# Segment attention of a two-layer kernel: a round's projection and the MLP of the round before it are issued between other work

## The reference

```python
xn = rms_norm(x, attn_norm_w)
q, k, v = split(xn @ to_qkv_w)
q, k = rope(q), rope(k)                      # t * cos + rh * sin, rh: neighbours swapped
kf, vf = [k_extra, pm, k], [v_extra, pm, v]  # prefix: memory and persistent tokens
probs = softmax(where(mask, q @ kf.T * DH**-0.5, -1e30))
x = x + (probs @ vf).merge_heads() @ to_out_w
a, g = split(rms_norm(x, ff_norm_w) @ ff_w1 + ff_b1)
x = x + silu(g) * a @ ff_w2 + ff_b2
```

## Time and profile before

| | us |
|---|---|
| median of 3 runs | 1343.94 |
| lowest and highest | 1338.87, 1344.26 |
| profiled execution: time, span | 1345.08, 1343.3 |
| segment stage's rounds in it | 997.1 to 1305.96 |
| last MLP | 1305.96 to 1343.3 |

### The profile page before, as it was taken

One profiled execution on the slowest core, in us unless ns is written; L12 is line 12 of the kernel. 1 busy time (PEld: TensorE's weight loads), 2 busy tenths in 40 slices (PEclk: granted clock), 3 DMA queues, 4 the chain that ended last, 5 costly groups with the idle time before them and its releaser, 6 DMA issues. The chain is left out here.

```text
span 1343.3 us, 38339 instructions
## 1 busy us (share of the span) xinstructions
PE 1169.8 (87%) x15980; PEld 795.3 (59%) x15980; DVE 928.7 (69%) x1742; ACT 747.0 (56%) x1029; POOL 847.5 (63%) x1227
## 2 busy tenths in 40 slices
PE   3888855899999999999999999998766887879775
PEld 2555544566666666666666666665443746456472
DVE  6778764777777777778787878777266375674632
ACT  2333333477777777777777777776512435344251
POOL 2455538878787878787888888851028294572830
PEclk9999866899999999999999999999877888989885
DMA  6200003323232323232223232211000000000000
GB/s 170 70 0 0 0 0 108 119 69 107 83 107 69 119 72 114 77 102 89 100 77 112 79 104 86 71 60 37 4 14 1 1 1 10 0 8 2 8 2 7
DMA packets 70398, 75.88 MB, mean 56 GB/s; under 512 B 21308, under 2 KB 64956, under 8 KB 70108
## 3 DMA queue, kind: packets, MB, share of 16 engines
q1 hardware_dynamic: 70236, 73.57, 17.3%
HBM read 32.90 MB, written 0.92 MB: 25 GB/s over the span
## 5 line engine op out<-in xcount | busy, mean ns | idle before, releaser
L928 DVE TENSOR_REDUCE tops_sb<-ps_b 112x2 f32<-112x1000 f32 x384 | 460.4, 1199 | 158.4 <-PE ps_b L778 155.7
L874 ACT ACTIVATE probs_sb<-ps_a 128x896 f32<-128x896 f32 x352 | 322.7, 917 | 118.5 <-PE ps_a L759 118.5
L750 PE MATMUL ps_d<-probs_sb,values_sb 128*32 128x112 f32 x6144 | 229.1, 267 | 0.6 <-ACT probs_sb L874 0.5
L778 PE MATMUL ps_b<-keys_sb,queries_sb 64*112 64x500 f16 x768 | 164.8, 420 | 16.6 <-DVE tops_sb L928 9.8
L217 POOL TENSOR_SCALAR context_sb<-context_sb,ln_sb 125x128 f32<-125x128 f32 x384 | 166.2, 449 | 7.6 <-POOL ln_sb L235 7.5
L750 PEld LDWEIGHTS ps_d<-probs_sb,values_sb 128*32 128x32 f32 x6144 | 135.5, 110 | 40.3 <-issue 7.5
L759 PEld LDWEIGHTS ps_a<-queries_sb,keys_sb 64*128 64x128 f16 x3072 | 125.2, 102 | 48.8 <-ACT probs_sb L874 8.1
L759 PE MATMUL ps_a<-queries_sb,keys_sb 64*128 64x112 f16 x3072 | 141.2, 210 | 4.7 <-ACT probs_sb L874 4.1
L806 PE MATMUL ps_c<-xs_t_sb,w_kv_sb 128*128 128x200 f32 (+1 forms) x384 | 127.4, 430 | 0.0
L815 PE MATMUL ps_c<-w_kv_sb,xs_t_sb 128*128 128x128 f32 x768 | 122.0, 297 | 5.1 <-ACT k_rows_sb L891 5.1
L815 PEld LDWEIGHTS ps_c<-w_kv_sb,xs_t_sb 128*128 128x128 f32 x768 | 97.9, 195 | 27.5 <-issue 21.9
(11 more groups left out here) (258 smaller groups left out, 1949.9 us busy)
## 6 DMA issues: line engine op xcount, KB each, us to landing
keys_sb<-k_split_sb SPq DMA_DIRECT2D x288, 125.0 KB, 2.5
context_sb<-in_ctx SPq DMA_DIRECT2D x32, 750.0 KB
queries_sb<-q_split_sb SPq DMA_DIRECT2D x24, 112.0 KB, 5.6
keys_sb<-in_ones SPq DMA_DIRECT2D x3, 375.0 KB, 4.5
w_qk_sb<-in_w_qkv SPq DMA_DIRECT2D x1, 1024.0 KB, 12.3
queries_sb<-shift_sb SPq DMA_DIRECT2D x64, 1.8 KB
x_all_sb<-in_x SPq DMA_DIRECT2D x2, 448.0 KB
queries_sb<-in_zeros SPq DMA_DIRECT2D x8, 112.0 KB, 5.5
```

The source lines that it names most:

```text
L750: last = nc.tensor.matmul(o_bank[32 * (g % 4):32 * (g % 4) + 32, 112 * (g // 4):112 * (g // 4) + 112], values[r][:, k, g, :], probs[k % 2] ...
L778: last = nc.tensor.matmul(ps_b[0:2 * T, 512 * e:512 * e + 500], queries_of(b + d, e, g), keys[(r + d) % 3][64 * e:64 * e + 64, g, 500 * u: ...
L874: nc.scalar.activation(probs[s % 2][:].rearrange("p (e n) -> p e n", e=2), halves(ps_a[:, :]), ACT.Exp).then_inc(Q["probs_ready"], 1)
L928: nc.vector.tensor_reduce(tops[(b + d) % 2][:, :, n // 3, n % 3], ps_b[0:2 * T, :].rearrange("p (e n) -> p e n", e=2)[:, :, 0:500], axis=A ...
```

## The change

Each engine's `emit` is taken apart into functions that are called in another order. A round is now scores and softmax first; then 16 steps n, in which stand slice n of the projection of round i + 1, the turned and weighted probabilities and the output of round i by the tables below, and the MLP of round i - 1. The value products of a round stand between its scores. Ahead of the loop stand the projection, turn and values of round 0, behind it the MLP of the last round. In the blocks below the removed lines are left out; they stand in the kernel above.

```diff
-UP_AT, HT_AT, DOWN_AT = (4, 8, 12), 3, 15
+TURNED = {0: ((0, 0), (0, 1)), 1: ((0, 2), (0, 3)), 2: ((1, 0), (1, 1)), 3: ((1, 2), (1, 3)), 5: ((2, 0), (2, 1)),
+          6: ((2, 2), (2, 3)), 8: ((3, 0), (3, 1)), 9: ((3, 2), (3, 3))}
+WEIGHTED = {2: ((0, 0),), 3: ((0, 1),), 5: ((1, 0),), 6: ((1, 1),), 8: ((2, 0),), 9: ((2, 1),), 11: ((3, 0), (3, 1))}
+HT_AT, UP_AT, DOWN_AT, OUT = 3, (4, 7, 10), 12, {13: (0, 1), 14: (2,), 15: (3,)}
+ROW_AT, Y_AT = 5, 14
```

GpSimd and VectorE:

```diff
+        rotate(0)
+        for i in range(NIT):
+            softmax(i)
+            if i + 1 < NIT:
+                rotate(i + 1)
...
+        memory_keys(0)
+        for n in range(16):
+            rotate(0, n)
+        for i in range(NIT):
+            softmax(i)
+            if i > 0:
+                mlp_normed(i - 1)
+            if i + 1 < NIT:
+                memory_keys(i + 1)
+            for n in range(16):
+                if i + 1 < NIT:
+                    rotate(i + 1, n)
+                if i > 0:
+                    mlp(i - 1, n)
+        mlp_normed(NIT - 1)
+        for n in range(16):
+            mlp(NIT - 1, n)
```

TensorE. The projections have two banks, the turned probabilities two (in quarters of four, `et_done` and `et_ready` count 16 a round), values and weighted share two, and the output lies in the MLP's bank 7; o1_t has four buffers:

```diff
+        def projected(i, n):
             wait = waiter3(pe, i)
+            if n >= 2:
+                wait("turn_read", n - 1)
+            elif i > 0:
+                wait("s_copied", 3, -1)
+            kind, j = slice_of(n)
+            nc.tensor.matmul(banks[n % 2][:, 0:NB * T], w_qk1[:, kind, 128 * j:128 * j + 128],
+                             xm[:, NB * i:NB * i + NB, 0:T], start=True, stop=True).then_inc(R["turn_done"], 1)
...
+        def scores(i, half, u):
+            wait = waiter3(pe, i)
+            if half == 0:
+                if u == 0:
+                    wait("turn_read", 16)
+                elif u == 1:
+                    wait("et_ready", 4 * U, -1)
+                else:
+                    wait("s_read", u - 1)
+            elif u < 2:
+                wait("s_read", u + 3)
+            else:
+                wait("s_copied", u - 1)
...
+        def turned(i, u, part):
+            wait = waiter3(pe, i)
+            if part == 0:
+                wait("e_normal", u + 1)
+            if u == 0 and part < 2:
+                wait("s_copied", U)
+            else:
+                wait("et_ready", 4 * u + part - 1)
+            for n in range(4):
+                last = nc.tensor.transpose(banks[2 + part % 2][0:NK1, 128 * n:128 * n + 128], s1[u][:, 4 * part + n, :], ident)
+            last.then_inc(R["et_done"], 1)
...
+        def out(i, u):
+            wait = waiter3(pe, i)
+            if u == 0:
+                wait("up_ready", 3, -1)
+            wait("o_ready", 2 * u + 2)
+            for j in range(NJ):
+                last = nc.tensor.matmul(banks[7][:, 128 * u:128 * u + 128], o1_t[u][:, j, :], w_out1[:, j, :],
+                                        start=(j == 0), stop=(j == NJ - 1))
+            last.then_inc(R["out_done"], 1)
...
+        for n in range(16):
+            projected(0, n)
+            if n % 2 == 1:
+                values1(0, n // 4, n // 2 % 2)
+        pe.wait_ge(persist_ready, 2)
+        pe.wait_ge(loaded_v, 16 * NB)
+        for i in range(NIT):
+            wait = waiter3(pe, i)
             for half in range(2):
                 wait("rotated", 8 + 8 * half)
                 for u in range(U):
+                    scores(i, half, u)
+                    if i > 0:
+                        values1(i, 2 * half + u // 2, u % 2)
+            for n in range(16):
+                if i + 1 < NIT:
+                    projected(i + 1, n)
+                for u, part in TURNED.get(n, ()):
+                    turned(i, u, part)
+                for u, half in WEIGHTED.get(n, ()):
+                    weighted(i, u, half)
+                if i > 0:
+                    mlp(i - 1, n)
+                for u in OUT.get(n, ()):
+                    out(i, u)
+        for n in range(16):
+            mlp(NIT - 1, n)
```

ScalarE:

```diff
+        for n in range(8):
+            values1(0, n // 2, n % 2)
+        for i in range(NIT):
+            wait = waiter3(act, i)
+            for u in range(U if i > 0 else 0):
+                values1(i, u // 2, u % 2)
             for u in range(U + 1):
                 if u < U:
                     wait("s_top", u + 1)
                     nc.scalar.copy(s1_view(u, 1), scores1(u)).then_inc(R["s_copied"], 1)
+                    if i > 0:
+                        values1(i, 2 + u // 2, u % 2)
                 if u > 0:
+                    exp1(i, u - 1)
+            for n in range(16):
+                for u, part in TURNED.get(n, ()):
+                    turned(i, u, part)
+                for u, half in WEIGHTED.get(n, ()):
+                    weighted(i, u, half)
+                if i > 0:
+                    mlp(i - 1, n)
+        for n in range(16):
+            mlp(NIT - 1, n)
```

More of the change, by code:

```diff
@@ L1097, in emit, with softmax @@
                             nc.gpsimd.tensor_tensor(dst, a[:], b[:], ALU.add).then_inc(R["rotated"], 1)
+                    def softmax(i):
+                        wait = waiter3(pool, i)
                         def normalise(u):
@@ L1145, in _ @@
                     pe.wait_ge(head_act, 4)
-                    def emit(i, mlp, attention):
+                    def projected(i, n):
                         wait = waiter3(pe, i)
[L1150 to L1198, removed]
-                        if not mlp:
-                            pe.wait_ge(persist_ready, 2)
-                            pe.wait_ge(loaded_v, 16 * NB)
@@ new lines, in mlp_turned, with mlp_up @@
+                    def mlp_turned(i):
+                        wait = waiter3(pe, i)
+                        wait("hn_ready")
+                        wait("y_ready", 1, -1)
+                        for u in range(U):
+                            last = nc.tensor.transpose(banks[6][:, 128 * u:128 * u + 128], normed[:, u, :], ident)
+                        last.then_inc(R["ht_done"], 1)
+                    def mlp_up(i, m):
+                        wait = waiter3(pe, i)
+                        if m == 0:
+                            wait("ht_ready")
+                        else:
+                            wait("up_ready", m)
+                        nc.tensor.matmul(banks[6], w_up1[:, m, :], h_t[:], start=True, stop=True)
+                        nc.tensor.matmul(banks[7], w_up1[:, 3 + m, :], h_t[:], start=True, stop=True
+                                         ).then_inc(R["up_done"], 1)
@@ new lines, in mlp_down @@
+                    def mlp_down(i):
+                        wait = waiter3(pe, i)
+                        wait("up_ready", 3)
+                        for u in range(U):
+                            for m in range(3):
+                                last = nc.tensor.matmul(banks[6][:, 128 * u:128 * u + 128], gate_e[:, m, 128 * u:128 * u + 128],
+                                                        w_down1[:, m, :], start=(m == 0), stop=(m == 2))
+                        last.then_inc(R["down_done"], 1)
@@ L1264, in emit @@
-                        weighted(U - 1)
-                        wait("et_ready", 2 * U)
-                        for u in range(U):
-                            wait("o_ready", 2 * u + 2)
-                            for j in range(NJ):
-                                last = nc.tensor.matmul(banks[3][:, 128 * u:128 * u + 128], o1_t[u % 2][:, j, :], w_out1[:, j, :],
-                                                        start=(j == 0), stop=(j == NJ - 1))
-                            last.then_inc(R["out_done"], 1)
@@ new lines, in mlp_normed @@
+                        link = tail[i][0]
+                        wait("out_done", U)
+                        nc.vector.tensor_tensor(h[:], banks[7].rearrange("p (u c) -> p u c", u=U),
+                                                x_all[:, U * i:U * i + U, :], ALU.add).then_inc(R["h_ready"], 1)
+                        wait("h_ready")
+                        for u in range(U):
+                            ins = nc.vector.bn_stats(st1[:, u, :], h[:, u, :])
+                        link(ins)
@@ L1447, in total, with softmax @@
+                    def softmax(i):
+                        wait = waiter3(ve, i)
+                        link, ends = main[i]
                         def total(u):
```

303 lines of the change are left out of this document (132 added, 171 removed).

## The result

The changed kernel takes 1336.61 us (median of 14, 1332.42 to 1340.22) against 1343.14 (median of 14, 1338.57 to 1345.52) for the kernel before: ratio 0.9956, interval 0.994 to 0.9971.

What follows compares the result with a forecast made beforehand. No engine was full; a round summed a GpSimd and a TensorE stretch. Period 32.5 + 43.1 = 75.6 us against 78.87; round 1 starts 1085.1, last output 1297.9, MLP 37.34: end 1335.2, forecast 1336, range 1325 to 1351.

Steps and rivals of the forecast that it cites:

- (a): Scores and softmax of a steady round: 3.8 us longer, last reciprocal at S+25.4 (S: the round's first scores).
- (b): VectorE's MLP norm and memory keys before the first rotary turn: 7.05 us as before, first slice ready at S+32.5.
- (c): TensorE stops at the third projection until VectorE reads the first: new 8.5 us stall; the earlier 4.40 us wait stays.
- (d): TensorE's work from S+32.5: 40.0 us, plus 2.15 clock restart and 0.95 handoffs, sum 43.1; period 75.6.
- (e): Round 0, with neither value products nor norm behind its softmax: round 1's first scores at 1085.1, 22.8 us earlier.
- (f): Last round, without projections: its output ends at S+61.3, with 0.3 us for the last drain, at 1297.9.
- (g): The last MLP, behind the last round: unchanged at 37.34 us, ending at 1335.2.
- The gates: Slower rival: ScalarE late at the MLP's up steps, TensorE idles and restarts at half clock; 1361 us, chance 0.13.
- Handoffs: Slower rival: a third of about 30 groups a round expose waits, 3 us in each of three rounds; 1345, chance 0.20.
- A softmax and a restart at no cost: Faster rival: softmax lengthening and clock restart don't come, 3.8 + 2.15 us in two rounds, 3.8 in the last; 1320, chance 0.10.
- GpSimd as the bound: Faster rival: GpSimd sets the period because TensorE's groups overlap more than shown; 60 us a round, 1305, chance 0.05.
- The rule weighed: GpSimd and VectorE share SBUF interfaces, so two-input norm operations may slow: at most 2.1 us a round, time 1340.

Runs made afterwards that it cites:

- the filled gap: Changed kernel plus 74 unused TensorE transposes in the stall before the third projection in rounds 1 and 2: 1333.75 us, ratio 0.9919.
- the longer turns: A GpSimd memset added to each of 16 rotary slices a round, in both kernels: kernel before 1361.05 us, changed kernel 1340.25 us.
- the values moved: Changed kernel with the second half's four value products and their ScalarE copies moved from the score units into steps 0 and 1: 1334.62 us, ratio 0.9942.
- both edits: Changed kernel with the MLP norm behind the first two rotary reads and the second half's value products in steps 0 and 1: 1321.53 us, ratio 0.985.
- the gaps filled: The kernel with both edits plus 22 unused transposes a round (40 in the last) behind the first projection: 1326.59 us, ratio 0.9875.

## Why the prediction was right, step by step

**(a) and (b), sums and first read.** The last reciprocal came at S+25.2 with its end (forecast 25.4), the third projection at S+32.1 (32.5). Within (a) two errors offset. A unit of scores with its value product took 1.97 us and not 1.86, so the second half's first maximum came at S+9.03 against S+7.11 before, 1.9 later where 1.5 stood; that leaves 1.7 for the second half, where 2.3 stood. (3.8 was no middle of its bounds of 0 and 6.1, but the sum of 1.5 and 2.3.)

**(c), the stall.** 8.35 and 8.59 us against 8.5, ended by the shuffle, as forecast. The wait before it, which was to stay at 4.40, was 2.48.

**(d), the sum.** 75.83 and 75.47 against 75.6. TensorE's part took 43.69, of which 2.26 is the clock (2.15 forecast) and 41.43 the rest (40.0 and 0.95 forecast); the filled gap returned 2.25 and 1.9 a round. GpSimd has room, and the longer turns show it: no us of them in steady rounds. But the room is 5.9 us and not 15: the forecast let GpSimd start at S+32.5 and run through, while its slices go at the pace of TensorE's sixteen steps. And TensorE was not "half idle" in the old GpSimd stretch: from 1155.46 to 1190.35 it was busy for 28.94 of 34.89 us, so that stretch had only 6 us of TensorE's time to give.

**(e), round 0.** 90.0 from the stage's start where 88.0 was forecast, the largest miss. The third projection came 0.8 early (53.9 from the stage's start, 54.8 forecast); from there to the next scores it was 36.0 us and not 33.2. These are the windows of that stretch in the changed kernel and in the one with the values moved, which has the same code there and the same wait of 2.21 us in front of it:

```profile
1048.50:1084.54 36.04, 36.04 (x397) 27.96 (x398) 17.52 (x45) 11.28 (x20) 32.49 (x32) 0.91 0.01 2
1049.38:1082.28 32.90, 32.90 (x396) 25.67 (x397) 17.56 (x45) 11.09 (x20) 31.72 (x31) 1.00 0.01 2
```

At the full clock it is 32.90, 1.3 above the 31.6 of the sum, and the lower clock adds 3.1, where 1.6 was charged. So the miss is half clock, half prices and handoffs. What makes the clock fall in one trace and not in the other, no run shows: with the same wait it was 32.90 in three traces and 36.0 to 37.1 in three others, and S1 lay between 86.8 and 91.1 in kernels with the same code of round 0.

**(f) and (g).** 61.40 to the output's end against 61.3 and 0.3. The last MLP was 1.1 shorter than in the profile before, at a granted clock of 0.67 against 0.58. In four later kernels with the same code it took 36.9 to 37.1, all at 0.58, so this is a level of the clock and not the change. It hides half of the miss in (e): that the whole stage came out at 338.8 us against 338.1 forecast is in part luck.

**The rivals.** The gates: 3.0 us of slack where 2.3 was reckoned, no wait; this rival is out. Handoffs at 3 us a round: no, 0.5 above the sum in a steady round and at most 1.3 in round 0, at the full clock. A softmax and a restart at no cost: no, both were there (3.6 and 2.3 us). GpSimd as the bound at 60 us a round: no, even with the norm out of the way the rounds stop at 69, with TensorE busy 63.5.

**The rule weighed.** One operation of the norm was caught by GpSimd's last normalisation, as the end of the sums (S+25.2) and GpSimd's end (S+27.4) let it. A pair of the sums, then that operation and the next:

```profile
1104.73 2.14 POOL L1101 TENSOR_TENSOR s_sb<-s_sb,s_sum_sb 128x1168 f32<-128x1168 f32 x1
1106.32 0.59 DVE L1492 SCALAR_TENSOR_TENSOR s_sum_sb<-s_sb,s_sum_sb 128x16 f32<-128x16 f32 x1
...
1109.81 2.14 POOL L1101 TENSOR_TENSOR s_sb<-s_sb,s_sum_sb 128x1168 f32<-128x1168 f32 x1 [0.40 <-DVE s_sum_sb L1494]
...
1111.63 0.34 DVE L1443 TENSOR_TENSOR ms_sb<-mv_sb 128x4 f32<-128x4 f32 x1
1112.00 0.16 DVE L1444 TENSOR_TENSOR ms_sb<-ms_sb,mv_sb 128x4 f32<-128x4 f32 x1
```

L1443 has two SBUF inputs and takes 0.34 us; L1444, of the same size but behind GpSimd's end, 0.16. The trace agrees in kind with the Trainium skill, GPSIMD Engine Reference, Specifications, on contention for two SBUF inputs, and the price here is 0.2 us a round, a tenth of the bound of 2.1. (Three rounds have a norm, so that bound stood for 1342, not 1340.)

The rows also show what sets the price. L1443 ends at 1111.97, 0.02 behind GpSimd's end (1111.95); L1492 above at 1106.91, 0.04 behind it (1106.87). All 16 instructions of that line in this trace, and all 16 in the trace before, end 0.02 to 0.04 us behind a GpSimd operation that ran when they began. So the 325 ns of the earlier trace rows were not "alone", as the prediction has it: that one began 0.29 us before GpSimd's end. The small operation is held until GpSimd's is over, and its price is what is left of GpSimd's. In the kernel with the norm behind the reads GpSimd rotates beside the norm, and two small operations are held in rounds 1 and 2 (the second has a single SBUF input):

```profile
1112.58 1.01 POOL L1092 TENSOR_TENSOR turn_b_sb<-turn_b_sb,const_sb 128x448 f32<-128x448 f32 x1
1112.77 0.83 DVE L1445 TENSOR_TENSOR ms_sb<-ms_sb,mv_sb 128x4 f32<-128x4 f32 x1
1113.66 1.14 POOL L1095 TENSOR_TENSOR q_sb<-turn_a_sb,turn_b_sb 128x448 f32<-128x448 f32 x1
1113.84 0.98 DVE L159 TENSOR_SCALAR ms_sb<-ms_sb 128x4 int32<-128x4 int32 x1
```

The norm takes 6.96 us there and 5.60 in the changed kernel. With both edits, where TensorE waits for it (0.70 us, and 2.06 with the gaps filled), it takes 6.95 to 7.16.

So the change moves a 35 us GpSimd stretch beside TensorE's work, without which a round takes 92.3 and not 75.8, but it also brings values into the softmax and leaves the norm ahead of a read on which an in-order TensorE now hangs. The net gain per round is 3.2 us. The 20.8 us that S1 comes early, because the MLP of round 0 now stands behind it, go back in the last round, which holds an MLP and has no rotary turns to hide.

## What to carry to other kernels

When two stretches are laid beside each other, look at the first instruction of the new neighbour that the in-order engine reaches: here one wait for a read behind a norm of 5.6 us held back 43 us of work, and putting the norm behind that read was worth as much (7.3 us, and 15.1 with the copies moved) as the whole rearrangement (6.5). What is pulled forward from the first round is pushed into the last, so count a pipelined loop by its steady period and by both ends. Filling a gap to hold the clock pays only where nobody else is late behind it: 2 us a round in one kernel, nothing in the next.

## What was not expected of the hardware

- Some small VectorE operations on SBUF (those with two inputs, and one with a single input) that meet a running GpSimd operation end only when that one ends: 0.16 us became 0.34 or 0.83, 0.17 became 0.98. The reductions of the sums (L1491) were not held: 1.31 to 1.37 us, beside GpSimd too.
- A 0.52 us memset on GpSimd between two dependent operations lengthened the pair by only 0.34 us.
- Behind a gap of 3.16 us the clock still fell to 0.50, after one group at full speed, and behind one of 3.26 it was down at once; behind 0.45 us it did not fall.
- Stretches of unchanged code differ between kernels: the first layer's end by 5.3 us, the last MLP by 1.1 with a clock of 0.58 or 0.67, the last round by 2.2 with 0.84 or 0.92, round 0 by 4.3, of which 3.1 to 4.2 come with a clock of 0.91 or 0.88 in place of 1.00. Single profiles don't tell 2 us at these places.
